# Criss-cross attention: when VectorE sums the energies of the last chunk pair, and when GpSimd clears Kg

## What is computed

```python
q = einsum('oc,bchw->bohw', Wq, x) + bq      # 64 channels
k = einsum('oc,bchw->bohw', Wk, x) + bk      # 64 channels
v = einsum('oc,bchw->bohw', Wv, x) + bv      # 512 channels
energy_H = einsum('bchw,bcgw->bhwg', q, k) - 1e30 * eye(H)   # along the column
energy_W = einsum('bchw,bchv->bhwv', q, k)                   # along the row
att = softmax(concatenate([energy_H, energy_W], -1), -1)
out = gamma * (einsum(v, att_H) + einsum(v, att_W)) + x
```

## Time and profile before

| | |
|---|---|
| time, median of 3 runs | 3690.41 us (3687.48 to 3691.53) |
| profiled execution, its own time | 3688.54 us |
| span of the profiled execution | 3686.8 us |
| TensorE matmuls busy | 3634.3 us, 99% of the span |
| VectorE, ScalarE, GpSimd busy | 73%, 51%, 26% |
| DMA | 237 GB/s, 77.7% of the 16 engines' time |

### The profile page before, as it was taken

The page is one execution under the profiler, slowest core; times in us unless marked ns, Lnnn a source line. Parts: engine busy times, 40 slices in busy tenths (PEclk is TensorE's granted clock), DMA queues, the critical chain, the costliest instruction groups (busy, mean ns, idle before and its releaser), DMA issues.

```text
span 3686.8 us, 67894 instructions
## 1 busy us (share of the span) xinstructions
PE 3634.3 (99%) x26296; PEld 3611.4 (98%) x26296; DVE 2677.8 (73%) x4326; ACT 1867.5 (51%) x3647; POOL 965.6 (26%) x1128
## 2 busy tenths in 40 slices
PE   8799999999999999999999999999999999999999
PEld 7799999999999999999999999999999999999999
DVE  7767787677876778767787677866778667786555
ACT  8525764257642676426754267542775427654111
POOL 1412243122431224202242022421224212342000
PEclk9899999999999999999999999999999999999999
DMA  8688868888698876977859787697776978769665
GB/s 273 171 237 259 267 199 244 230 269 261 196 250 238 262 259 195 257 238 260 261 176 269 236 264 256 181 266 242 257 250 199 263 242 258 237 207 256 210 208 181
DMA packets 333966, 874.01 MB, mean 237 GB/s; under 512 B 34640, under 2 KB 186704, under 8 KB 333648
## 3 DMA queue, kind: packets, MB, share of 16 engines
q1 hardware_dynamic: 333648, 869.67, 77.7%
HBM read 661.92 MB, written 207.62 MB: 236 GB/s over the span
## 4 chain that ended last, share of the span: by engine, by line
PE 96%; DVE 2%; issue 0%; DMA 0%; ACT 0%; POOL 0%; SPq 0%; DVEq 0%; ACTq 0%; POOLq 0%
PE bank L1134 44%; PE bank L1101 19%; PE bank L1122 18%; PE bank L1032 10%; PE bank L1068 3%; PE bank L1054 2%; DVE Sy L772 1%; DVE E L793 0%; PE bank L1086 0%; PE bank L1029 0%; PE bank L1042 0%; DMA e_scratch<-E 0%; DVE Y L872 0%; DVE mx_c L788 0%; ACT Sy L650 0%
## 5 line engine op out<-in xcount | busy, mean ns | idle before, releaser
L1134 PE MATMUL bank<-Sy,Wv_hi 128*128 128x384 f32 x6144 | 1588.6, 339 | 3.6 <-DVE Sy L772 3.6
L1134 PEld LDWEIGHTS bank<-Sy,Wv_hi 128*128 128x128 f32 x6144 | 1090.1, 189 | 7.2 <-issue 4.8
L1134 PE MATMUL bank<-Sy,Wv_lo 128*128 128x384 f32 x3072 | 1030.6, 335 | 0.0
L881 DVE SCALAR_TENSOR_TENSOR Y<-bank,bv_sb,Y 128x384 f32<-128x384 f32 x768 | 466.3, 612 | 405.4 <-PE bank L1134 404.4
L1122 PE MATMUL bank<-Pt,XT 128*128 128x96 f32 x6144 | 717.3, 274 | 0.3
L1122 PEld LDWEIGHTS bank<-Pt,XT 128*128 128x128 f32 x6144 | 713.7, 192 | 1.6 <-DVE Y L872 1.5
L1101 PE MATMUL bank<-Pt,XT 128*128 128x96 f32 x6144 | 690.4, 276 | 1.0 <-issue 1.0
L1101 PEld LDWEIGHTS bank<-Pt,XT 128*128 128x128 f32 x6144 | 689.6, 193 | 1.2 <-issue 1.2
L650 ACT ACTIVATE Sy<-Y 128x768 fp32r<-128x768 f32 x384 | 311.9, 838 | 687.1 <-PE bank L1134 649.2
L1134 PEld LDWEIGHTS bank<-Sy,Wv_lo 128*128 128x128 f32 x3072 | 579.0, 188 | 0.0
L477 POOL TENSOR_TENSOR Pe<-Pe,F 128x384 f32<-128x384 f32 x336 | 279.8, 835 | 1076.9 <-DMA Pe<-e_scratch 1041.5
(11 more groups left out here) (83 smaller groups left out, 3122.6 us busy)
## 6 DMA issues: line engine op xcount, KB each, us to landing
XT<-in_x_col SPq DMA_DIRECT2D x384, 384.0 KB, 5.7
XT<-in_x_row SPq DMA_DIRECT2D x384, 384.0 KB, 5.9
Y<-in_x SPq DMA_DIRECT2D x192, 768.0 KB, 6.6
out<-Y SPq DMA_DIRECT2D x184, 768.0 KB, 4.4
XA<-in_x SPq DMA_DIRECT2D x180, 768.0 KB, 5.0
e_scratch<-E SPq DMA_DIRECT2D x384, 144.0 KB, 3.0
Pe<-e_scratch SPq DMA_DIRECT2D x336, 144.0 KB, 5.4
XA_first<-in_x SPq DMA_DIRECT2D x12, 768.0 KB, 6.3
```

Source lines behind the costliest of these rows:

```text
L881: nc.vector.scalar_tensor_tensor(at, proj_ps[c % 2][:, 0:CP], bv_sb[:, c:c + 1], at, op0=ALU.add, op1=ALU.add).then_inc(out_made, 1)
L1134: last = nc.tensor.matmul(proj_ps[c % 2][:, 0:CP], w[:, ct, at], Sy[:, lo, ct, :], start=(ct == 0 and k == 0), stop=(ct == CT - 1 and k == 2))
```

## The change

`add_energies` of the first of the two chunks of position 17 (chunk 22) moves from behind the second `add_row` to ahead of the last tile's `finish`. `zero_kg` moves from the start of position 18 to position 17, ahead of the subtractions of chunk 23. In its old place GpSimd now waits for both halves of `low_y` of chunk 18 before it gathers.

```diff
 (GpSimd, row_stage)
                     if b_now and b_now[0] == 0:
-                        zero_kg(b + 1)
+                        pool.wait_ge(y_lo_made, past(y_lo_made, (b * CHUNKS + n + 1) * HALVES))
                         gather_k(b + 1, 0)
                         gather_k(b + 1, 1)
                         zero_q(b + 1)
...
                     if n + 4 < CHUNKS:
                         scale(b, CHUNKS + n + 4)
+                    if more and n == A_LAST:
+                        zero_kg(b + 1)
                     if a_now:
 (VectorE, row_stage)
                     if turn_now:
                         turn(b + 1, 0)
+                    if more and n == A_LAST:
+                        add_energies(b + 1, a_now[0])
                     if n + 2 < CHUNKS:
                         finish(b, n, 3)
                         low_y(b, n + 1, 0)
                         add_row(b, n + 2, 0)
                         low_y(b, n + 1, 1)
                         add_row(b, n + 2, 1)
-                        if a_now:
+                        if a_now and n < A_LAST:
                             add_energies(b + 1, a_now[0])
```

## The result

The changed kernel takes 3668.2 us in the median of 5 runs (3667.01 to 3669.72) against 3688.78 us (3687.05 to 3691.53, 5 runs) for the kernel before; the ratio is 0.9944 with a 95% interval of 0.993 to 0.9959. That is 20.6 us or 0.56% less, nearly three times what a measurement of this kernel can tell from no change.

The account below looks back on a forecast made before the run. TensorE was taken as the bound, with work in 3634.3 of 3686.8 us. Seven windows totalling 69.34 us shrink to 6.85 us each, 21.4 us less: 3690.41 - 21.4 = 3669.0 us, range 3664 to 3678.

Parts of the forecast that it names:

- the low clock: Projection after TensorE's wait ran at 1.2 GHz in five of seven batches, 3.67 us; forecast at full clock, about 2.1 us.
- the break: TensorE idles 1.74 us in batch 1 before chunk 23's row energies, awaiting VectorE's sum; forecast gone, 11.6 us over seven.
- what the sum did not have: Forecast sum covered seven windows, attention of chunk 19 to project(18, 1): 69.34 us less 7 x 6.85, 21.4 us gained.
- The cover: VectorE's idle gap before the last finish, 1.84 us, takes the moved sum's 1.51 us at no cost, 0.33 spare.
- that rival: project(18, 0) stays at 1.2 GHz in five batches, costing 1.67 us each, 8.3 in all: 3677.3 us; chance 0.10.
- The clearing: Clearing Kg, 0.73 us, moves into GpSimd's 3.47 us wait for ScalarE; costs nothing and alone gains nothing.
- The wait: GpSimd's gather waits for low_y, whose second half then takes 0.94 us, gaining 0.51 us in six batches.
- The interval: Attention of chunk 19 to project(18, 1): 3.49 + 0.20 + 2.46 + 0.62 = 6.77 us, taken as 6.85.
- Row (19, 3): Fourth attention row of chunk 19; TensorE's wait ahead of it was forecast to stay at 0.20 us.
- the energies with the projection: Chunk 23's energies plus one projection at full clock on TensorE, taken as 2.46 us of the interval.
- a wait at column group 0: TensorE waits for VectorE's sum of chunk 23 before the column energies; taken as 0 to 0.1 us.
- Nothing should be given back: After the windows everything follows TensorE, busy without a break, so none of the 21.4 us should be lost.

Follow-up runs that it names:

- filled: Kernel before, with 9 useless matmuls into a free bank ahead of the row energies of chunk 23, keeping TensorE busy while it waits: 3681.88 us, ratio 0.9983.
- sum_only: Kernel before with only VectorE's half of the change, the sum of chunk 22 ahead of the last finish: 3670.79 us, ratio 0.9953.
- no_wait: Changed kernel without the gather's new wait for low_y; the clearing and the sum stay moved: 3668.88 us, ratio 0.9945.
- low_first: Changed kernel with the first half of low_y of chunk 18 ahead of the finish of tile 3 at position 17: 3667.46 us, ratio 0.9941.
- gpsimd_only: Kernel before with only GpSimd's half of the change, Kg cleared early and the gather's wait; sum unmoved: 3678.78 us, ratio 0.9974.

## Why the prediction was right

The forecast was 3669.0 us and a range of 3664 to 3678; 3668.2 was measured. The mechanism held: VectorE's sum was what held TensorE, and the low clock came with the break. That the two numbers are only 0.8 us apart is in part luck: the forecast started from a median of 3690.41 us in three runs, where five runs gave 3688.78, and this 1.6 us made up for much of what the sum did not have (the last point below). The gain was forecast as 21.4 us and measured as 20.6.

- **The break.** Right: the wait of L1054 for L805 (11.6 us, seven times) is gone from TensorE's list, and no other input of the energies came late.
- **The cover.** I counted 1.84 us of idle, 1.51 us of work and 0.33 us to spare. The trace has 0.33 us left.
- **The low clock.** I counted it as gone with the break and gave its staying 0.10. It is gone in all seven batches, and `filled` shows the tie, which the trace of before could not. The price of 1.67 us per batch in that rival was slightly high: batch 1 against batch 6, which has the same break at full clock, gives 1.54.
- **GpSimd's edits.** The clearing was costed at 0 and is 0, apart from the 0.3 us of batch 3 whose cause is open. The wait was credited with 0.51 us of `low_y` in six batches. The size is right against `sum_only`, where the gather runs into `low_y`; but with the clearing moved as well, the wait itself saves only 0.20 us of `low_y` (`no_wait`). I had valued it in the order of before. That the second half takes 0.94 us in all batches was wrong for batch 3, where it takes 1.28.
- **The interval.** I took 6.85 us; it is 6.92 to 6.95 in six batches and 6.64 in batch 3, 6.90 in the mean. Two terms were too small. Row (19, 3) is released late, and I counted the 0.20 us of idle time for that; it costs 0.29, the difference between 3.78 us to the energies in six batches and 3.49 in batch 3 and in `low_first`. And the energies with the projection take 2.53 us, where I had 2.46, because right behind the attention the energies take 0.41 us (505.49 to 505.90) and not the 0.35 that they take between two projections. The 0.08 us that I put in for a wait at column group 0 covered the second by chance: TensorE's list has no such wait. In batch 3 VectorE was ahead of the second subtraction (1403.74 against 1403.81), so row (19, 3) came in time.
- **What the sum did not have.** In the profiles, the time up to the attention of batch 1's position 17 was 1.0 us shorter and the rest 3.3 us longer, nearly all of it in the stretches between batches that are told apart above. "Nothing should be given back" was wrong by that much in this execution. It is why the idle time fell by 9.0 us and not by the 12 that I wrote; the busy time fell by 9.8, where I had 8 to 9 for the low clock, which is 7.7 of it.

## What to carry to other kernels

Price an idle stretch of TensorE by what follows it as well: here five of six breaks of 1.7 us were followed by another 1.5 us of loss at half clock (10.42 us against 8.88), and even useless matmuls in the break paid. Where two engines wait for each other, look for work that is ready early but stands late in an in-order list; the gap it can fill is where its engine waits for the bound. Where VectorE and GpSimd both read SBUF, it was the one that started second that grew longer in all the pairs above, so let the one that the bound waits for start first.

## What the runs showed of the hardware

- A break of 1.7 us of TensorE was followed by a fall of the clock to 1.2 GHz in five of six batches (kernel before), one of 1.2 us in one of seven (`gpsimd_only`), and one of 1.2 us in batch 3 of the kernel before, below, was not; with filler in the break there was no fall in seven. The same break at the same place of the program does not always have the same effect: batch 6 of the kernel before kept the full clock through 1.74 us.

```profile
1414.67 0.57 PE L1054 MATMUL bank<-k_split,q_split 128*96 128x192 f32 x4 [1.22 <-DVE E L805]
```

- VectorE's subtraction of 768 columns takes 0.94 us alone and 1.09 to 1.61 when a GpSimd instruction that reads SBUF was running first. The length depends on how much of that one was left: the subtraction ends 0.81 to 0.83 us after GpSimd's end, as if it had waited for it (502.45 + 1.61 against 502.24 + 0.99 in the changed kernel, 506.01 + 1.14 against 504.75 + 1.57 in `no_wait`, 1405.07 + 1.28 against 1403.81 + 1.73 in batch 3). When VectorE is first, GpSimd's takes 1.55 to 1.73 instead of 0.84 to 0.99. Beside a running clearing of Kg the subtraction is not lengthened.
